# A decoder layer on one core: the second transpose of each row group moves from its own PSUM bank to the two dense banks, and three engines' orders with it

## The reference, cut to what matters

```
x1 = layernorm(x  + self_attention(x))               # no softmax, so linear in each batch
x2 = layernorm(x1 + cross_attention(x1, ctx, mask))  # 16 heads of 32, 154 context rows, softmax
xr = mu_r * x2 + (1 - mu_r) * x2_prev                # x2_prev: x2 shifted by one row
xk = mu_k * x2 + (1 - mu_k) * x2_prev
y  = sigmoid(xr @ W_r.T) * (relu(xk @ W_k.T)**2 @ W_v.T)
out = layernorm(x2 + y)
```

## Time and profile before

| | |
|---|---|
| time, median of 3 runs | 938.97 us (938.12 to 940.32) |
| the profiled execution | 940.32 us, span 938.2 us |
| PE busy | 912.5 us, 97% of the span, 6676 matmuls |
| DVE, ACT, POOL busy | 667.9, 552.4 and 515.4 us (71%, 59%, 55%) |
| mean granted clock of PE over the span | 0.994 |
| DMA | mean 49 GB/s, 45.64 MB |

### The profile page before, as it was taken

How to read it: one execution, slowest core, us unless ns; L and a number is a source line. 1 busy time by engine, 2 the same in 40 slices (tenths; PEclk the granted TensorE clock), 3 DMA queues, 4 the chain that set the end, 5 groups by cost and what they waited for, 6 DMA issues and landing times.

```text
span 938.2 us, 18936 instructions
## 1 busy us (share of the span) xinstructions
PE 912.5 (97%) x6676; PEld 729.4 (78%) x6676; DVE 667.9 (71%) x1979; ACT 552.4 (59%) x1654; POOL 515.4 (55%) x507
## 2 busy tenths in 40 slices
PE   5999999998999999999999999999999999999997
PEld 5877657666788888887878787878787878787876
DVE  6487554556686877777777777777777777777775
ACT  6455305657675757575656575757575656666631
POOL 1034015657676666666566666675757584847421
PEclk9999999999999999999999999999999999999999
DMA  8593010102110101011100010010101010100001
GB/s 279 187 303 137 23 25 24 42 1 73 48 30 24 30 24 30 24 30 67 43 24 30 24 28 26 16 39 9 45 8 46 8 46 9 45 2 23 2 23 45
DMA packets 30872, 45.64 MB, mean 49 GB/s; under 512 B 2747, under 2 KB 15547, under 8 KB 30523
## 3 DMA queue, kind: packets, MB, share of 16 engines
q1 hardware_dynamic: 26123, 35.26, 11.7%
q10 hardware_dynamic: 4656, 9.18, 2.8%
HBM read 34.10 MB, written 9.70 MB: 47 GB/s over the span
## 4 chain that ended last, share of the span: by engine, by line
PE 77%; DVE 5%; issue 2%; ACT 2%; POOL 0%; POOLq 0%; DVEq 0%; ACTq 0%
PE dense L87 18%; PE dense L89 17%; PE dense L88 17%; PE turned L1450 6%; PE scores L1438 5%; PE rest_value L1464 4%; PE rest_value L1468 3%; PE dense L1350 2%; PE rest_value L1456 1%; PE turned L1350 1%; PE dense L1394 1%; PE scores L1356 1%; DVE mix_k_raw L1049 1%; DVE prob L1009 1%; ACT prob L744 1%
## 5 line engine op out<-in xcount | busy, mean ns | idle before, releaser
L1259 POOL TENSOR_TENSOR row_inv<-row_sum,minus_one 128x4 f32<-128x4 f32 x128 | 141.8, 1108 | 249.7 <-ACT prob L744 246.6
L744 ACT ACTIVATE prob<-prob,row_min 128x154 f32<-128x154 f32 x512 | 209.9, 418 | 16.8 <-DVE row_min L1009 16.8
L1265 POOL TENSOR_TENSOR prob<-prob,row_inv 128x512 f32<-128x512 f32 x128 | 147.0, 1148 | 0.0
L1009 DVE CUSTOM_DVE_ANT_0 prob<-scores,mask_add 128x154 f32<-128x154 f32 x512 | 129.3, 310 | 6.6 <-PE scores L1438 6.4
L752 ACT ACTIVATE prob_t<-turned 128x512 f32<-128x512 f32 x128 | 76.1, 595 | 61.8 <-PE turned L1450 60.5
L744 ACT ACTIVATION_READ_ACCUMULATOR prob<-prob,row_min 128x1 f32 x512 | 98.9, 193 | 0.0
L1016 DVE TENSOR_TENSOR o_t_lo<-rest_value,o_t_hi 128x256 fp32r<-128x256 f32 x64 | 26.9, 420 | 83.8 <-ACT o_t_hi L763 83.8
L1450 PE MATMUL turned<-ident,prob 128*128 128x128 f32 x512 | 79.4, 278 | 0.4 <-POOL prob L1265 0.4
L763 ACT ACTIVATE o_t_hi<-rest_value 128x256 fp32r<-128x256 f32 x64 | 24.5, 382 | 88.2 <-PE rest_value L1468 88.2
L87 PE MATMUL dense<-xt_hi,cross_wq_hi 128*128 128x256 f32 x256 | 74.2, 290 | 1.3 <-DVE xt_lo L1000 1.3
L87 PE MATMUL dense<-mix_k_hi,ffn_wk_hi 128*128 128x256 f32 x256 | 75.2, 294 | 0.0
(11 more groups left out here) (266 smaller groups left out, 2602.7 us busy)
## 6 DMA issues: line engine op xcount, KB each, us to landing
x_rows<-x_rows SPq DMA_DIRECT2D x32, 256.0 KB, 4.7
xt_raw<-x_cols SPq DMA_DIRECT2D x16, 512.0 KB, 3.7
out<-gate_then_y SPq DMA_DIRECT2D x15, 512.0 KB, 2.8
mask_in<-mask SPq DMA_DIRECT2D x16, 154.0 KB, 2.3
cross_wv<-cross_wv SPq DMA_DIRECT2D x1, 1024.0 KB, 9.1
cross_wk<-cross_wk SPq DMA_DIRECT2D x1, 1024.0 KB, 9.7
self_wv<-self_wv ACTq DMA_DIRECT2D x1, 1024.0 KB, 5.6
self_wk<-self_wk ACTq DMA_DIRECT2D x1, 1024.0 KB, 10.4
```

Source lines behind the costliest of these rows:

```text
L744: m = act.activation(keys, keys, ACT.Exp, bias=row_min[:, buf, t, h:h + 1], scale=-1.0, accum_out=row_sum[:, buf, t, h:h + 1])
L1009: m = dve.tensor_tensor_reduce(prob[buf][:, t, h * CTX:(h + 1) * CTX], s_bank[:, h, t * CTX:(t + 1) * CTX], mask_add[n % 2][:, t, :], -SCA ...
L1259: pool.tensor_tensor(row_inv[:, buf, t, :], row_sum[:, buf, t, :], minus_one[:], ALU.pow).then_inc(*p_inv.up)
L1265: pool.tensor_tensor(keys[:, :, 0:P], keys[:, :, 0:P], inv.broadcast_to([P, HPG, P]), ALU.mult).then_inc(*p_norm.up)
```

## The change

Six things change together. (1) The two turns of x2 go through d0 and d1, and the waits that guard these banks and `t_bank` are changed to match. (2) On PE `r_product(e,1)` moves behind both turns of x2, and the second turn of x2 moves in front of the first turn of x1. (3) On ACT `r_gate(e,1)` moves behind `turned_x2(f,1)`, and `mix_high(f,"r")` moves in front of `exponentials(n,3,0)`. (4) On DVE `difference(f)` and `blend(f,"r")` move in front of `x1t_low(a,0)`. (5) On POOL `r_mix_low(f)` moves in front of `weigh(n,3,0)`. (6) `transposes(n,2,0)` no longer waits for x2. No instruction is added or dropped, and the written-out last group keeps its order.

```diff
-        two = {... "x2": (t_bank, t_bank), ...
+        two = {... "x2": (d0, d1), ...
 # ACT
                 if live(e):
                     r_gate(e, 0)
-                    r_gate(e, 1)
                 if live(f):
                     turned_x2(f, 0)
                 if live(n):
                     o_high(n, 1)
-                x1t_high(a, 0)
                 if live(f):
                     turned_x2(f, 1)
+                if live(e):
+                    r_gate(e, 1)
+                x1t_high(a, 0)
                 x1t_high(a, 1)
                 if live(n):
                     take_turned(n, 2, 0)
+                if live(f):
+                    mix_high(f, "r")
+                if live(n):
                     exponentials(n, 3, 0)
                 if live(e):
                     k_relu_half(e, 1)
-                if live(f):
-                    mix_high(f, "r")
 # DVE
                 if live(n):
                     o_low(n, 1)
+                if live(f):
+                    difference(f)
                 if a:
                     make_mask(a)
+                if live(f):
+                    blend(f, "r")
                 x1t_low(a, 0)
                 if live(n):
                     masked_min(n, 3, 0)
                 x1t_low(a, 1)
 ...
-                if live(f):
-                    difference(f)
-                    blend(f, "r")
 # POOL
-                if live(n):
-                    weigh(n, 3, 0)
                 if live(f):
                     r_mix_low(f)
                 if live(n):
+                    weigh(n, 3, 0)
                     weigh(n, 3, 1)
 # PE, waits
             def x1_turn(n, t):
                 pe.wait_ge(*ln_ok[1].at(n, t + 1))
-                if n >= 3:
-                    pe.wait_ge(*r_out.at(n - 3, t + 1))
-                elif n == 2 and t == 0:
-                    pe.wait_ge(*fm_out.at(0, 3))
-                else:
-                    pe.wait_ge(*y_sum.at(n, t + 1))
+                if t == 0 and n >= 2:
+                    pe.wait_ge(*x2t_out.at(n - 2, 2))
+                elif t == 0 and n == 1:
+                    pe.wait_ge(*y_sum.at(n, 2))
+                if t == 1 and n >= 3:
+                    pe.wait_ge(*r_out.at(n - 3, 2))
+                elif t == 1 and n == 2:
+                    pe.wait_ge(*x2t_out.at(0, 1))
 # transposes
-                if u == 2 * TPG and 0 < n < LAST:
-                    pe.wait_ge(*x2t_out.at(n - 1))
 # x2_turn
-                elif n == LAST - 1:
+                elif t == 0:
+                    pe.wait_ge(*y_sum.at(n + 2, 2))
+                elif n:
                     pe.wait_ge(*r_out.at(n - 1, 1))
-                elif t == 0:
-                    pe.wait_ge(*t_out.at(n + 1, 2 * TPG))
                 else:
-                    pe.wait_ge(*x2t_out.at(n, 1))
+                    pe.wait_ge(*fm_out.at(0, 3))
 # r_product
-                elif n == LAST - 2:
+                elif t == 0:
+                    pe.wait_ge(*y_sum.at(n + 3, 1))
+                else:
                     pe.wait_ge(*x2t_out.at(n + 1, 1))
-                else:
-                    pe.wait_ge(*y_sum.at(n + 3, t + 1))
 # PE, order
                 if live(e):
                     r_product(e, 0)
-                    r_product(e, 1)
                 if live(f):
                     x2_turn(f, 0)
                 if live(n):
                     values(n, 1)
-                x1_turn(a, 0)
                 if live(f):
                     x2_turn(f, 1)
+                if live(e):
+                    r_product(e, 1)
+                x1_turn(a, 0)
                 if live(n):
                     scores(n, 3)
                 x1_turn(a, 1)
```

More of the change, by code:

```diff
@@ L606, in layers @@
         row_min, row_sum, row_inv = (mem.place(x, [P, 2, TPG, HPG]) for x in ("row_min", "row_sum", "row_inv"))
-        two = {"y": (d1, d0), "x1": (d1, d0), "q": (d0, d1), "o": (d1, d0), "x2": (t_bank, t_bank), "k": (d0, d1), "r": (d1, d0),
+        two = {"y": (d1, d0), "x1": (d1, d0), "q": (d0, d1), "o": (d1, d0), "x2": (d0, d1), "k": (d0, d1), "r": (d1, d0),
                "v": (d0, d1)}
```

## The result

The changed kernel takes 948.30 us (median of 4 runs, 947.26 to 949.38), the kernel before beside it 938.55 us (938.01 to 940.32). The ratio is 1.0092, with a 95% interval of 1.0077 to 1.0108: slower by 0.9%. The forecast was 945.8 us with a range of 941.0 to 949.5. The profiled execution of after took 948.29 us, its span is 946.2 us; the one of before took 940.32, its span is 938.2. So the two profiles lie 8.0 us apart and the medians 9.75. The profiles can explain the 8.0. Over all 21 executions of after on record the median is 947.26, so the four above are a little on the slow side.

The account below looks back on a forecast made before the run. PE was taken to bound the kernel. Full rounds +5.3, round 1 +3.1 and round 6 -2.2 made +6.2 us, 940.32 to 946.5 on the profiled execution; 945.8 us was said for the median, range 941.0 to 949.5.

Parts of the forecast that it names:

- What bounds the kernel, and the one tight place: PE is busy 613.12 of 615 us in rounds 2 to 14; k's second half has 0.60 us of room behind `x1t_low`.
- The stream of PE, +0.02 us a round: PE's own steps from r to k, without waits, take 9.85 us against 9.83 before: +0.02 (-0.04 to +0.13).
- The wait before k, 0.42 us: Each full round, k waits for `x1t_low` behind r's blend: lags 0.20, 1.59, 0.69, 0.06 make 2.54 against PE's 2.12.
- Nothing else is hit by the moved steps: What queues behind the waiting blend on DVE, and the moved POOL step, make nothing else late.
- Round 1, +3.1 us: q starts 3.0 us later, 2.1 of it kept; a clock drop adds 1.0; together +3.1 us (1.5 to 4.7).
- Round 6, -2.2 us: The value product's 1.88 us wait shrinks to about 0.8, and the clock gives 1.5: -2.2 us (-0.5 to -2.5).
- The sum: Whole kernel: 5.3 + 3.1 - 2.2 = +6.2 us on the profiled execution, 940.32 to 946.5; 945.8 said for the median.
- No wait before k: Rival: the 0.42 us wait in full rounds goes, leaving +1.1 us, so 940.1 us; chance 0.12.
- The clock falls in the full rounds: Rival: the clock drops in half of the full rounds at 1.7 us each, 12 more, about 958 us; chance 0.08.
- Faster: Rival: round 6's wait and clock loss vanish, round 1's delay is absorbed, k doesn't wait; 935.4 us; chance 0.05.
- What was to show it: k's first matmul waits for DVE `xt_lo` about 13 times, about 0.4 us each, 5 in total; blends of r 48.1 apart.
- The shared port: DVE with two SBUF inputs and GpSimd reading SBUF alternate; the moved blend misses POOL, k's blend is freed; sum stays 5.3.

## Why the prediction was right, and where its sizes were off

- **What bounds the kernel, and the one tight place: right.** PE has no other new wait in the full rounds than k's. All the room worked out for the two turns of x2, the value product and the second half of r was there: none of them shows a wait.
- **The stream of PE, +0.02 us a round: right, but for another reason.** The steps measured are 2.89 for half of r (350.71 to 353.60), 0.53, 1.00, 0.41 for the turn in front of r (0.42 was taken), 2.88, 0.53, 0.74, 0.49 and 0.36 (the last one from before, since k waits here), together 9.83 us, which is what before had: the stream itself costs nothing. Rounds in which k shows no wait took 47.70 us, +0.02, and there k started 9.87 us behind r, 0.04 late, at its lag behind `x1t_low`. That the number came out is luck.
- **The wait before k, 0.42 us: right in kind, too small.** It is 0.58. Two of the four terms were taken from other instructions. "Starts 0.20 us after PE has gone on" came from ACT; DVE's blend starts 0.28 after (358.42 to 358.70). "PE starts 0.06 us after such an end" came from q; k starts 0.14 after (360.98 to 361.12), and the experiment with one wait fewer shows that 0.08 of it is the second semaphore. 1.59 + 0.69 were exact. Together 0.28 + 1.59 + 0.69 + 0.14 = 2.70, and 2.70 - 2.12 = 0.58. A full round costs 0.58 where 0.44 was said, over twelve rounds 1.7 us more, the largest error of the sum.
- **Nothing else is hit by the moved steps: right but for round 2.** There k starts 10.59 us behind r instead of 10.41, and the round takes 0.15 us longer. POOL starts a multiplication at 260.10 while DVE subtracts, DVE's conversion of the mask at 261.15 takes 1.16 us instead of its usual 0.31, and the blend comes at 262.22 only:

```profile
259.91 1.31 DVE L1041 TENSOR_TENSOR diff<-x_t 128x1024 f32<-128x1024 f32 x1
261.15 1.16 DVE L970 TENSOR_SCALAR mask_add<-mask_in 128x308 f32<-128x308 int32 x1
262.22 1.66 DVE L1051 SCALAR_TENSOR_TENSOR mix_r_raw<-diff,cols,x_t 128x256 f32<-128x256 f32 x4
```

```profile
260.10 2.03 POOL L1268 TENSOR_TENSOR prob<-prob,row_inv 128x512 f32<-128x512 f32 x1
```

  The prediction had looked for a meeting of the moved *blend* with POOL, in a later round, and found none. It hadn't looked at the moved difference, nor at round 2, where POOL works at another time. The same slow conversion stands in round 2 of all seven profiles with the new order of PE in which it comes between the difference and the blend or `x1t_low`. With the mask behind the blend it takes 0.32 us and the round's extra loss is gone, so the conversion beside POOL's multiplication is the cause. That the shared port is what the two meet at is only read from the durations (1.04 is what L1268 takes alone).
- **Round 1, +3.1 us: right.** It is +3.5. The wait of q was to be near 4 us; it is 2.74, since the turn of x1 in front of it already waits 0.78 for ACT's copy of x2, a wait that the prediction didn't have. It came from putting x1 behind the second copy of x2 without asking what lies between them in a round that has no r. The clock was to cost 1.0; the first half of q takes 4.23 us (218.81 to 223.04) where it took 2.97 before (216.68 to 219.65), so 1.26. The value product's wait at the end gives back 0.5 (1.05 us instead of 1.57), where the prediction had 0.9. So the sum of +3.1 owes its accuracy partly to errors that cancel, and to an execution in which the clock fell.

```profile
213.68 0.63 PE L1352 MATMUL dense<-ident,x 128*128 128x128 f32 x4 [0.78 <-ACT x_t L788]
...
218.81 0.58 PE L87 MATMUL dense<-xt_hi,cross_wq_hi 128*128 128x256 f32 x1 [2.74 <-DVE xt_lo L1002]
...
223.04 0.60 PE L1452 MATMUL turned<-ident,prob 128*128 128x128 f32 x4
```

- **Round 6, -2.2 us: right.** It is -1.9. The wait of the value product was to be near 0.8 and is 0.85, and the clock stays up: the k product behind it takes 3.04 us (477.58 to 480.62), and from 470 to 490 us the granted clock is 1.00. Before, that product took 4.54 (472.67 to 477.21). The terms are -1.50 for the clock, as said, -1.03 for the wait of the value product and +0.58 for k's wait, where -1.09 and +0.44 were said. The 1.50 is gained only against an execution in which the clock had fallen in round 6, as it had in the profile of before.

```profile
476.58 0.64 PE L1466 MATMUL rest_value<-prob_t,v_rest 128*32 128x256 f32 x8 [0.85 <-ACT prob_t L757]
...
477.58 0.39 PE L87 MATMUL dense<-mix_k_hi,ffn_wk_hi 128*128 128x256 f32 x1
```

```profile
470.00:490.00 20.00, 19.14 (x127) 15.55 (x126) 18.73 (x56) 11.26 (x42) 13.35 (x14) 1.00 0.08 31
```

- **The sum.** +6.2 was forecast for the profiled execution, and it is +8.0: 11 x 0.14 = 1.5 for k's wait, 0.3 for round 2, 0.4 for round 1 and 0.3 for round 6, less 0.6 by which the start of the kernel was quicker in this execution: 1.9, against the 1.8 measured. That the medians lie 9.75 apart and not 8.0 fits the remark that the profiled run of before was its slowest: against the 938.55 of the median the change costs more than against the 940.32 of that run. The median of 945.8 that was forecast is 2.5 us below the 948.30, and 1.5 below the 947.26 of all executions.
- **The rivals.** No wait before k: excluded by the 13 waits of k; it needed 0.42 us of error. The clock falls in the full rounds: it didn't, at 1.00 over 374 us, but the kernel with only DVE's order shows that it was a real danger: with waits of 2.75 us it fell in most rounds. Faster: excluded with the first.
- **What was to show it.** "About 13 times, about 0.4 each, 5 in total" against 4.6 us in the page, and yet the wait costs more, since the view's idle time begins at the modelled end. The spacing of the blends was the better test: 48.26 us against the 48.1 that was said, and 580.03 from the first to the last against 578.
- **The shared port.** The moved blend takes 1.68 us in the full rounds, as long as before, so it doesn't meet POOL there, and the blend of k takes 2.6 us instead of 3.59: both as said.

## What to carry to other kernels

A product that is split so that its two halves stand apart ends later, and everything that waits for its *end* moves with it. Look for what stands in the queue behind the instruction that waits for that end: here `x1t_low` had no need of r, but stood behind a blend that did, and one swap of two lines of DVE's order gave back 0.56 us of each round. Price such a wait by the distance of starts, add up the lags between engines for the very pair of engines and waits, and go through the first rounds separately, where some of the groups are missing and cover is gone.

## What the runs showed of the hardware

- A second semaphore wait in front of a matmul, on a value that had long been there, cost 0.08 to 0.09 us: k started 0.14 us after the end it waited for, and 0.05 with one wait fewer.
- DVE began 0.28 us after PE had gone on from the product it waited for, where ACT began after 0.20 (358.42 on PE, 358.70 on DVE, 358.62 on ACT). Whether it is the engine or its waits that makes the difference wasn't tested.
- The same blend of four instructions took 2.6 us with POOL's new order, and 3.59 (before) or 4.71 (DVE's new order) with POOL's old one, where one alone takes 1.6 to 1.7.
- A conversion on DVE with one SBUF input took 1.16 us instead of 0.31 behind a subtraction on DVE and beside a multiplication on POOL that itself took 2.03 instead of 1.04. In the profile with that conversion moved away the multiplication still took 2.03, so that length isn't the conversion's doing.
- The granted clock stayed at 1.00 with an idle time of 0.35 us in each round (0.57 with the mask moved, where rounds were evenly 48.50 us), and behind the waits of 1.24 to 1.26 us of round 6 in three profiles. It fell in round 6 behind waits of 1.88 and 2.13 us. Behind waits of 2.74 to 2.88 us in round 1 it fell in three profiles and stayed at 1.00 in two.
- In the kernel with only DVE's order it fell in most of the rounds with an idle time of 2.75 us, to 0.79 over the 8 us around it. Its matmuls then ran at 0.41 instead of 0.28 us, at the lower level (1.2 GHz) for some 3 us, and this cost about 1.4 us in most rounds and 2.7 in two; two rounds paid nothing.
